# Latent attention with key-major scores and four heads per group, in place of turned probabilities

## The chip, the cores and the metric

The kernel runs on one core of one Trainium2 chip. The metric is the device time of one launch in microseconds. Engines: TensorE (PE, with its weight loads as PEld), VectorE (DVE), ScalarE (ACT), GpSimd (POOL), and SyncE (SP), which issues most DMA transfers. SP's transfers share one queue that is served by the core's 16 DMA engines.

## The reference, cut to what matters

A decoder of two layers works on x of 2 sequences x 1024 tokens x 256 channels. Only the first block is touched by the change, the latent attention of layer 0 (16 heads of 16 channels):

```python
q, k, v = x @ Wq, x @ Wk, x @ Wv                  # x after a layernorm
latent_kv = (k + v) @ W_down_kv                   # 64 latent channels
k_rec, v_rec = latent_kv @ W_up_k, latent_kv @ W_up_v
scores = einsum('bhqd,bhkd->bhqk', heads(q), heads(k_rec)) / 16
scores = clip(scores, -1e4, 1e4)
scores = scores * exp(-1e-4 * abs(i - j))         # i query, j key position
scores = clip(scores, -1e4, 1e4)
out = einsum('bhqk,bhkd->bhqd', softmax(scores), heads(v_rec)) @ Wo
```

The result is added to x. Cross attention, a ternary feed-forward net, feature attention, a second cross attention and routed experts follow; they are as before.

## The kernel before, in words

The program is a row of blocks. Each block holds one instruction list per engine, engines wait for one another by semaphores, and a block ends when all its engines have. Around the change stand, in this order, `normalise`, `latent_projections`, `latent_attention` and `project_out`. The names P = 128, S = 1024, G = 512 (four tiles of 128 tokens), QT = 8 tiles per sequence, HD = 16, H = 16, D = 256 and B = 2 are used throughout.

`latent_projections` makes q and k with channels on the partitions, in 16 pieces of 128 channels x 512 tokens. ScalarE and VectorE split each piece into three bf16 parts whose sum is the fp32 value (L422, L383, L429, L390), and SP stores the parts in DRAM (L445) as `q_parts` and `k_parts`. VectorE takes the largest magnitudes (L385), from which a flag `inside` tells that no score can reach the clip.

`latent_attention` walks over 16 heads x 2 sequences x 8 query tiles, 256 tiles. For each head and sequence, SP loads 12 transfers of 16 rows (L537, L541) into stacks of 96 rows: the six products of parts that count, so that one bf16 matmul gives scores of nearly fp32 precision. Per tile:

- TensorE makes 128 queries x 1024 keys of scores (L578, two matmuls of 512 columns).
- VectorE multiplies by the decay table and takes the maximum of the row in the same instruction (L659, which the profile lists as a custom operation); GpSimd negates that maximum (L563).
- ScalarE takes exp with the negated maximum as bias and sums the row (L706).
- TensorE turns the probabilities, eight fp32 transposes of 128x128 (L588); ScalarE and VectorE copy them from PSUM (L521, L519).
- TensorE multiplies the turned probabilities by the values (L603), four query tiles beside each other in four column groups of 32. This is software pipelined three to eight tiles behind the scores.

Every fourth tile the result is turned back (L612) and divided by the sums (L637, L640). When `inside` is 0 a path with explicit clipping runs instead; the inputs here take the path without it. Last in GpSimd's list stands `clear_slots`, which writes 5 MB of zeros to DRAM (L114, L116), for the routed experts much later.

Of the kernel before, what the change touches and what calls it, by code (L numbers as in the profile page):

```python
# [21 lines left out]
P = 128  # L22
# [279 lines left out]
def latent_projections(k, v_heads, q_scratch, k_scratch):  # L302
# [5 lines left out]
    qk_ready, part1_done, rest1_done, part2_done, part3_done = (  # L308
        k.sem("qk_ready"), k.sem("part1_done"), k.sem("rest1_done"), k.sem("part2_done"), k.sem("part3_done"))
    v_ready, v_done = k.sem("v_ready"), k.sem("v_done")  # L310
    bound_own, largest_ready, largest_turned = k.sem("bound_own"), k.sem("largest_ready"), k.sem("largest_turned")
    stored = [k.sem(f"stored{s}") for s in range(4)]
    scale = 1.0 / 16.0
    NP = NG * 2 * KD
    with ExitStack() as c, nc.Block() as block:
# [3 lines left out]
        parts = k.sb(c, "parts", [P, 4, 3, G], BF16)  # L319
# [7 lines left out]
        def _(pe):  # L327
# [16 lines left out]
            for g in range(NG):  # L344
                rows = slice(g * G, (g + 1) * G)
                for m in range(KD):
                    n = 4 * g + m
                    wait(pe, rest1_done, n - 3)
                    for kd in range(KD):
                        last = pe.matmul(k.ps[:, m, :], k.w["L0_attn_Wq"][:, kd, m * P:(m + 1) * P],  # L350
                                         k.xt[:, kd, rows], start=kd == 0, stop=kd == KD - 1)
                    last.then_inc(qk_ready, 1)
                pe.wait_ge(lat_done, g + 1)
                for m in range(KD):
                    n = 4 * g + 2 + m
                    wait(pe, rest1_done, n - 3)
# [15 lines left out]
        def _(dve):  # L372
# [4 lines left out]
            for g in range(NG):  # L377
                for n in range(4 * g, 4 * g + 4):
                    s = n % 4
                    dve.wait_ge(part1_done, n + 1)  # L380
                    wait(dve, part2_done, n - 3)
                    wait(dve, part3_done, n - 3)
                    dve.scalar_tensor_tensor(out=rest[:, s, :], in0=k.ps[:, s, :], scalar=scale if s < 2 else 1.0,  # L383
                                             in1=parts[:, s, 0, :], op0=ALU.mult, op1=ALU.subtract).then_inc(rest1_done, 1)
                    own.did(dve.tensor_reduce(largest[:, n:n + 1], parts[:, s, 0, :], AX, ALU.max, apply_absolute_value=True))  # L385
                for n in range(4 * g, 4 * g + 4):
                    s = n % 4
                    dve.wait_ge(part2_done, n + 1)
                    dve.wait_ge(rest1_done, n + 1)
                    dve.tensor_tensor(parts[:, s, 2, :], rest[:, s, :], parts[:, s, 1, :],  # L390
                                      ALU.subtract).then_inc(part3_done, 1)

# [15 lines left out]

        @block.scalar  # L410
        def _(act):
# [3 lines left out]

            copy_latent(0)
            for g in range(NG):
                for n in range(4 * g, 4 * g + 4):
                    s = n % 4
                    act.wait_ge(qk_ready, n + 1)  # L420
                    wait(act, stored[s], 16 * g)
                    act.activation(parts[:, s, 0, :], k.ps[:, s, :], ACT.Copy,  # L422
                                   scale=scale if s < 2 else 1.0).then_inc(part1_done, 1)
                if g + 1 < NG:
                    copy_latent(g + 1)
                for n in range(4 * g, 4 * g + 4):
                    s = n % 4
                    act.wait_ge(rest1_done, n + 1)
                    act.activation(parts[:, s, 1, :], rest[:, s, :], ACT.Copy).then_inc(part2_done, 1)  # L429
                for t in range(g * TPG, (g + 1) * TPG):  # L430
                    b, q = divmod(t, QT)
                    act.wait_ge(v_ready, t + 1)
                    act.activation(v_heads[:, b * H:(b + 1) * H, q, :],
                                   k.ps[:, 5 + t % 2, 0:D].rearrange("p (h d) -> p h d", d=HD),
                                   ACT.Copy).then_inc(v_done, 1)

        @block.sync
        def _(sp):
            for n in range(NP):
# [3 lines left out]
                scratch = q_scratch if s < 2 else k_scratch  # L443
                sp.wait_ge(part3_done, n + 1)
                sp.dma_start(scratch[:, b * D + m * P:b * D + (m + 1) * P, half * G:(half + 1) * G]  # L445
                             .rearrange("c p n -> p c n"), parts[:, s, :, :]).then_inc(stored[s], 16)
            for s in range(4):
                sp.wait_ge(stored[s], 16 * NG)

def latent_attention(k, v_heads, attn, decay, q_scratch, k_scratch):

    nc = k.nc
    k.next_block()
    stack_in = [k.sem(f"stack_in{u}") for u in range(2)]
    scored, clipped, peaked, shifted = (  # L460
        k.sem("scored"), k.sem("clipped"), k.sem("peaked"), k.sem("shifted"))
    exp_done, v_staged = k.sem("exp_done"), k.sem("v_staged")
    p_turned = [k.sem(f"p_turned{u}") for u in range(2)]
    pt_done = [k.sem(f"pt_done{u}") for u in range(2)]
    mixed, mix_copied, mix_turned, inverted, weighted = (
        k.sem("mixed"), k.sem("mix_copied"), k.sem("mix_turned"), k.sem("inverted"), k.sem("weighted"))
# [8 lines left out]
    with ExitStack() as c, nc.Block() as block:  # L475
# [18 lines left out]

        def steps(eng, step):

# [1667 lines left out]
```

## Time and profile before

| | |
|---|---|
| median of 3 runs | 1616.47 us (1616.34 to 1617.06) |
| profiled execution, its own time | 1615.76 us |
| its span | 1614.2 us |
| projections block | about 22 to 84 us |
| attention block | 84 to 622 us |
| PE / DVE / ACT / POOL busy over the span | 83% / 57% / 58% / 12% |

In the rows below, times are microseconds from the start of the span. A row of the timeline gives start, duration, engine, line, operation, tiles, shapes, the count of merged instructions, and in brackets how long the engine was idle before and what ended that.
### The profile page before, as it was taken

Reading aid. Unit: us, or ns where it says so; the run is one execution under the profiler, and the core shown is the slowest. Engines: PE = TensorE matmul, PEld = TensorE weight load, DVE = VectorE, ACT = ScalarE, POOL = GpSimd, SP = SyncE. Lnnn points to the kernel's source line nnn. Section 1 sums busy time; section 2 is a strip of 40 time slices with the busy share of each in tenths; the row PEclk is TensorE's granted clock in tenths of the full one; section 3 lists DMA queues with packets and bytes.
Section 4 is the critical chain, followed back from the end, with each engine's and each line's share of the span. In section 5 each row is a group of like instructions: output and inputs, shape, how many; then the busy total and the mean of one; then the engine's idle time right before and its main releaser. Section 6 shows DMA issues by size and latency. Waiting matters only on the chain. (4 is left out here: it accounts for less than half of the span.)

```text
span 1614.2 us, 36474 instructions
## 1 busy us (share of the span) xinstructions
PE 1340.0 (83%) x12288; PEld 960.2 (59%) x12291; DVE 919.8 (57%) x2059; ACT 930.1 (58%) x1793; POOL 190.5 (12%) x546
## 2 busy tenths in 40 slices
PE   5879999999999995898365699889874489999992
PEld 2347777777777774544223464364354279999992
DVE  5558888888888873532788844563354223323233
ACT  2469999999999991355375377624631033333330
POOL 0001111111111110111200000031120701111110
PEclk9879999999999997899756899988995589999996
DMA  3311010010101013200000100033006211111115
GB/s 115 131 51 31 22 27 24 24 26 23 29 20 29 20 38 110 80 1 4 16 1 0 31 1 1 1 120 129 1 4 212 102 34 36 37 36 38 36 33 166
DMA packets 60025, 74.30 MB, mean 46 GB/s; under 512 B 13006, under 2 KB 47728, under 8 KB 59952
## 3 DMA queue, kind: packets, MB, share of 16 engines
q1 hardware_dynamic: 53168, 56.76, 11.9%
q0 software_dynamic: 4672, 14.50, 2.7%
q10 hardware_dynamic: 2112, 2.10, 0.4%
q8 instruction: 43, 0.70, 0.2%
q14 instruction: 30, 0.25, 0.0%
HBM read 50.43 MB, written 22.88 MB: 45 GB/s over the span
## 5 line engine op out<-in xcount | busy, mean ns | idle before, releaser
L659 DVE CUSTOM_DVE_ANT_0 probs_sb<-banks,decay_sb 128x1024 f32<-128x1024 f32 x256 | 308.2, 1221 | 43.6 <-PE banks L578 22.5
L706 ACT ACTIVATE probs_sb<-probs_sb,shift_sb 128x1024 f32<-128x1024 f32 x256 | 294.8, 1151 | 18.1 <-POOL shift_sb L563 16.4
L588 PEld LDWEIGHTS banks<-ident_sb,probs_sb 128*128 128x128 f32 x2048 | 238.3, 141 | 55.1 <-issue 22.9
L588 PE MATMUL banks<-ident_sb,probs_sb 128*128 128x128 f32 x2048 | 267.8, 274 | 0.9 <-ACT probs_t_sb L521 0.8
L521 ACT ACTIVATE probs_t_sb<-banks 128x512 f32<-128x512 f32 x384 | 214.7, 597 | 4.1 <-PE banks L588 2.3
L578 PE MATMUL banks<-k_stack_sb,q_stack_sb 96*128 96x512 bf16 x512 | 156.9, 389 | 14.0 <-DMA k_stack_sb<-k_parts 10.7
L603 PE MATMUL banks<-probs_t_sb,v_head_sb 128*32 128x128 f32 x4096 | 151.2, 277 | 0.7 <-ACT probs_t_sb L521 0.7
L1846 PEld LDWEIGHTS banks<-slots_xt_sb,tile_w_sb 128*128 128x128 f32 x1248 | 146.5, 193 | 1.9
L1846 PE MATMUL banks<-slots_xt_sb,tile_w_sb 128*128 128x128 f32 x1248 | 146.6, 276 | 0.0
L1858 PE MATMUL banks<-experts_w_sb,xt_sb 128*128 x624 | 141.2, 379 | 1.3 <-issue 1.3
L1892 ACT ACTIVATE slots_xt_sb<-banks 128x256 f32<-128x256 f32 x39 | 14.9, 383 | 213.8 <-PE banks L1832 213.8
L1858 PEld LDWEIGHTS banks<-experts_w_sb,xt_sb 128*128 128x128 f32 x624 | 115.5, 190 | 15.8 <-issue 1.7
L519 DVE COPY probs_t_sb<-banks 128x512 f32<-128x512 f32 x128 | 88.6, 692 | 57.7 <-PE banks L588 56.0
L603 PEld LDWEIGHTS banks<-probs_t_sb,v_head_sb 128*32 128x32 f32 x4096 | 100.3, 109 | 32.3 <-issue 31.4
L563 POOL TENSOR_TENSOR shift_sb<-peak_sb,minus_sb 128x1 f32<-128x1 f32 x256 | 48.5, 190 | 452.8 <-DVE peak_sb L659 452.8
L977 DVE TENSOR_REDUCE peak_sb<-banks 128x8 f32<-128x616 f32 x64 | 49.9, 798 | 87.8 <-PE banks L826 87.8
L1019 ACT ACTIVATE pt_sb<-banks,keyfill_sb 77x1024 f32<-77x1024 f32 x64 | 67.5, 1104 | 38.0 <-PE banks L857 37.1
L1902 ACT ACTIVATE xt_sb<-banks,tile_b_sb 128x128 f32<-128x128 f32 x312 | 84.7, 387 | 5.1 <-PE banks L1846 3.4
L1942 DVE COPY tile_w_sb<-experts_w_sb 128x2048 f32 x39 | 47.8, 1227 | 60.2 <-issue 28.0
L1927 DVE TENSOR_TENSOR is_best_sb<-slots_x_sb,tile_owned_sb 128x1 f32<-128x1 f32 x39 | 6.2, 159 | 122.2 <-DMA outputs_y<-slots_y_sb,output_row_sb 122.2
L253 POOL TENSOR_TENSOR x_sb<-x_sb,bb_sb 128x256 f32<-128x256 f32 x48 | 33.0, 732 | 337.2 <-DMA bb_sb<-in_L_attn_bo 276.7
L1881 POOL DMA_INDIRECT outputs_y<-slots_y_sb,output_row_sb x39 | 37.4, 959 | 258.7 <-DVE slots_y_sb L1955 154.0
(289 smaller groups left out, 1910.0 us busy)
## 6 DMA issues: line engine op xcount, KB each, us to landing
experts_w_sb<-in_L_ffn_W SPq DMA_DIRECT2D x16, 1024.0 KB, 11.9
q_stack_sb<-q_parts SPq DMA_DIRECT2D x192, 32.0 KB, 1.7
k_stack_sb<-k_parts SPq DMA_DIRECT2D x192, 32.0 KB, 1.8
slots_x<-zeros_sb POOLq DMA_DIRECT2D x1, 5031.0 KB, 22.6
slots_x_sb<-slots_x SPq DMA_DIRECT2D x39, 129.0 KB, 2.1
xt_sb<-outputs_y SPq DMA_DIRECT2D x8, 512.0 KB, 5.5
q_parts<-parts_sb SPq DMA_DIRECT2D x8, 384.0 KB, 3.0
k_parts<-parts_sb SPq DMA_DIRECT2D x8, 384.0 KB, 4.2
```

Of the source, the lines that this page charges most:

```text
L519: ins = eng.tensor_copy(dst, k.ps[:, 4 + half, :])
L521: ins = eng.activation(dst, k.ps[:, 4 + half, :], ACT.Copy)
L578: last = pe.matmul(k.ps[:, 2 * (s % 2) + half, :], qs[:, u, q * P:(q + 1) * P], ks[:, u, half * 512:(half + 1) * 512], start=True, stop=True)
L588: last = pe.transpose(k.ps[:, 4 + half, j * P:(j + 1) * P], pr[:, s % 4, (half * TPG + j) * P:(half * TPG + j + 1) * P], k.ident[:, :])
L603: last = pe.matmul(k.ps[32 * j:32 * j + 32, 6, 0:P], vh[:, u, kt, :], pt[:, j, gs % 2, kt, :], start=kt == 0, stop=kt == QT - 1)
L659: dve.tensor_tensor_reduce(out=pr[:, s % 4, :], in0=scores, in1=decay[:, off:off + S], scale=1.0, scalar=-3.0e38, op0=ALU.mult, op1=ALU.ma ...
L706: act.activation(pr[:, s % 4, :], pr[:, s % 4, :], ACT.Exp, bias=shift[:, s % 8:s % 8 + 1], accum_out=sums[:, (s // TPG) % 4, s % 4:s % 4 ...
L977: dve.tensor_reduce(peak[:, t % TPG, 2 * half:2 * half + 2, :], k.ps[:, bank:bank + 2, 0:SLOTS * C].rearrange("p r (s n) -> p r s n", n=C) ...
L1019: act.activation(pt[:, n % 2, 2 * half:2 * half + 2, :], k.ps[0:C, 2 * half:2 * half + 2, :], ACT.Exp, bias=key_fill[:, b:b + 1]).then_inc ...
L1846: last = pe.matmul(k.ps[:, 2 * u + f // HALF, (f % HALF) * P:(f % HALF + 1) * P], w1[:, u, kd, f * P:(f + 1) * P], xst[:, u, kd, :], start ...
L1858: last = pe.matmul(k.ps[:, 6, s * D:(s + 1) * D], ht[:, s, f, :], r.w2[:, bass.ds(e, 1), f, :].rearrange("p a n -> p (a n)"), start=f == 0 ...
L1902: ins = act.activation(ht[:, s, f, :], k.ps[:, 2 * s + f // HALF, (f % HALF) * P:(f % HALF + 1) * P], ACT.Gelu_apprx_tanh, bias=b1[:, s, f ...
```

## The change

In `latent_projections`, q and k are each stored in two versions, multiplied by exp(-c n) and exp(+c n) with n the position, so that the product of one version of q with the other of k already carries the decay on one side of the diagonal. That makes 32 rounds instead of 16. GpSimd takes the third part's subtraction. The stacks of the first group are loaded during the last rounds, and the decay tables are loaded here instead of in `normalise`.

In `latent_attention`, work goes in 16 groups: four heads of one sequence x 512 queries. Scores are made twice. The first product, query tile by query tile, serves only to find each row's maximum (`highest`, VectorE; its multiplied scores go to a tile nobody reads); it runs 22 tiles ahead. The maxima of a group are split in three bf16 parts by GpSimd, turned by TensorE, copied, and stored by one transfer as three more rows of the query stack, against rows of -1 in the key stack. The second product has the keys on the partitions, 128 keys x 512 queries, and comes out with the maximum subtracted; ScalarE takes exp of it straight from PSUM and TensorE multiplies it by the values without a turn. A column of ones in the values gives the sums. On diagonal tiles both sides of the diagonal are made and GpSimd's `affine_select` zeroes the wrong half of each. The weights' columns are reordered on the host so that four heads lie together.

Core of the diff (the attention functions are new, so they are shown as they are after it):

```diff
 def latent_projections(k, v_heads, fade_in, stacks, later):
...
+            def apply_fade(e):
+                n, version = divmod(e, 2)
+                dve.wait_ge(qk_ready, n + 1)
+                wait(dve, part3_done, e - 3)
...
+                dve.scalar_tensor_tensor(out=rest[:, e % 4, :], in0=k.ps[:, n % 4, :], scalar=scale if is_query(e) else 1.0,
+                                         in1=fade[:, side, half * G:(half + 1) * G],
+                                         op0=ALU.mult, op1=ALU.mult).then_inc(faded, 1)
+            def subtract_first(e):
...
+        @block.gpsimd
+        def _(pool):
+            for e in range(NV):
+                pool.wait_ge(part2_done, e + 1)
+                pool.wait_ge(rest1_done, e + 1)
+                pool.tensor_tensor(parts[:, e % SLOTS, 2, :], rest[:, e % 4, :], parts[:, e % SLOTS, 1, :],
+                                   ALU.subtract).then_inc(part3_done, 1)
...
+            def first_part(e):
+                act.wait_ge(faded, e + 1)
+                wait(act, stored[e % SLOTS], 16 * (e // SLOTS))      # SLOTS = 6
+                act.activation(parts[:, e % SLOTS, 0, :], rest[:, e % 4, :], ACT.Copy).then_inc(part1_done, 1)
...
+            for e in range(NV):                                      # SP; NV = 32
+                sp.wait_ge(part3_done, e + 1)
+                rows = slice(b * D + m * P, b * D + (m + 1) * P)
+                sp.dma_start(scratch[version, :, half, rows, :].rearrange("c p n -> p c n") if s < 2 else
+                             scratch[version, :, rows, half * G:(half + 1) * G].rearrange("c p n -> p c n"),
+                             parts[:, e % SLOTS, :, :]).then_inc(stored[e % SLOTS], 16)
+                if e == 19:
+                    for x in range(SLOTS):
+                        sp.wait_ge(stored[x], 16 * len(range(x, 16, SLOTS)))
+                if 20 <= e < 26:
+                    load_stacks(sp, stacks, 0, e - 20)
...
+def load_stacks(eng, stacks, g, piece):
+    n, half = divmod(g, 2)
+    b, first = divmod(n * HEADS, H)
+    rows = slice(b * D + first * HD, b * D + (first + HEADS) * HD)
+    version, r = divmod(piece, 3)
+    copies, row = 3 - r, HD * [0, 3, 5][r]
+    dst = slice(row, row + copies * HD)
+    if half == 0:
+        eng.dma_start(stacks.k[dst, n % 2, version, :, :].rearrange("p h n -> p (h n)"),
+                      stacks.k_scratch[version, 0:copies, rows, :].rearrange("c (p h) n -> c p (h n)", h=HEADS)).then_inc(stacks.arrived[g % 3], 16)
+    eng.dma_start(stacks.q[dst, g % 3, version, :, :].rearrange("p h n -> p (h n)"),
+                  stacks.q_scratch[version, r, half, rows, :].rearrange("(p h) n -> p (h n)", h=HEADS)
+                  .unsqueeze(0).to_broadcast([copies, HD, HEADS * G])).then_inc(stacks.arrived[g % 3], 16)
...
 def latent_attention(k, v_heads, attn, decay, inner, stacks):
...
+    GROUPS = 2 * B * H // HEADS      # 16
+    TILES = HEADS * TPG              # 16
+    LEAD = 6
+    TURN_STEP = 5
...
+            def store_peaks(g):
+                sp.wait_ge(peaks_copied, g + 1)
+                sp.dma_start(stacks.q[ROWS:ROWS + PARTS, g % 3, :, :, :].rearrange("p v h n -> p (v h n)"),
+                             peak_rows[:, g % 2, :]).then_inc(peaks_in, 16)
+            for g in range(1, 3):
+                for piece in range(6):
+                    load_stacks(sp, stacks, g, piece)
+            store_peaks(0)
+            for g in range(1, GROUPS):
+                store_peaks(g)
+                if g + 2 < GROUPS:
+                    sp.wait_ge(key_scored, g * UNITS)
+                    for piece in range(6):
+                        load_stacks(sp, stacks, g + 2, piece)
...
+            def scores(tile):                       # TensorE: for the maxima, 1024 columns in 2 or 3 matmuls
+                g, x = divmod(tile, TILES)
+                h, j = divmod(x, TPG)
+                if x == 0:
+                    stacks_arrived(pe, stacks, g)
+                wait(pe, peaked, tile - 1)
...
+            def key_scores(g, i, h):                # TensorE: 128 keys x 512 queries, banks 4 to 6 in a ring
+                if i == 0 and h == 0:
+                    pe.wait_ge(peaks_in, (g + 1) * 16)
+                wait_for_bank(pe, item)
...
+            def sum_values(s):
+                pe.wait_ge(exp_done, unit_index(g, i, HEADS if on_diagonal(i) else HEADS - 1) + 1)
+                if on_diagonal(i):
+                    pe.wait_ge(selected, s // 2 + 1)
...
+            pe.wait_ge(constants, 2)
+            for tile in range(TILES + LEAD):
+                scores(tile)
+                if tile == TILES + 1:
+                    turn_peaks(0)
+            for g in range(GROUPS):
+                for i in range(QT):
+                    if g * QT + i >= 2:
+                        sum_values(g * QT + i - 2)
+                    for x in range(2):
+                        for h in range(2 * x, 2 * x + 2):
+                            key_scores(g, i, h)
+                        if x == 1 and i == TURN_STEP and g + 1 < GROUPS:
+                            turn_peaks(g + 1)
+                        if tile_at(g, i, x) < GROUPS * TILES:     # (g + 1) * TILES + 2 * i + LEAD + x
+                            scores(tile_at(g, i, x))
+                    if on_diagonal(i):                            # i odd
+                        diagonal_scores(g, i)
+                    if i == 3 and g > 0:
+                        turn_mix(g - 1)
...
+        def _(pool):
+            own.did(pool.memset(vh[:, :, :, :, :], 0.0))          # 128 x 2048 fp32
+            own.wait()
+            pool.memset(stacks.k[ROWS:ROWS + PARTS, :, :, :, :], -1.0).then_inc(constants, 1)   # 3 x 16384 bf16
+            pool.wait_ge(constants, 1)
+            pool.tensor_copy(ident_b[:, :], k.ident[:, :]).then_inc(constants, 1)
...
+            def select(g, i):
+                pool.wait_ge(exp_done, unit_index(g, i, HEADS - 1) + 1)
+                pool.affine_select(later, later, [[0, HEADS], [1, P]], ALU.is_ge, 0.0, base=0, channel_multiplier=-1)
+                pool.wait_ge(exp_done, unit_index(g, i, HEADS) + 1)
+                pool.affine_select(earlier, earlier, [[0, HEADS], [-1, P]], ALU.is_gt, 0.0, base=0,
+                                   channel_multiplier=1).then_inc(selected, 1)
...
+            def exponential(g, i, h):                             # ScalarE, 576 times 128 x 512
+                act.wait_ge(key_scored, u + 1)
+                act.wait_ge(released, u + 1)
+                act.activation(out, k.ps[:, bank_of((exp_done, u + 1)), :], ACT.Exp).then_inc(exp_done, 1)
```

Values are multiplied two steps after their exps. The stacks have three slots for queries and two for keys. A group with an even number loads both, one with an odd number only queries.

## Rows read from the trace of the kernel before

**Rows 1.** The page's part 1: busy time and share of the span.

```profile
PE 1340.0 (83%) x12288; PEld 960.2 (59%) x12291; DVE 919.8 (57%) x2059; ACT 930.1 (58%) x1793; POOL 190.5 (12%) x546
```

**Rows 2.** Busy time in the attention loop, with its columns.

```profile
core 0: us, PE busy (x) PEld busy (x) DVE busy (x) ACT busy (x) POOL busy (x), PEclk, DMA share, GB/s
...
92.00:608.00 516.00, 509.02 (x6718) 375.47 (x6716) 412.60 (x768) 496.98 (x960) 58.90 (x289) 0.99 0.11 27
```

**Rows 3.** Timeline of PE in steady state.

```profile
299.93 0.61 PE L578 MATMUL banks<-k_stack_sb,q_stack_sb 96*128 96x512 bf16 x2
300.38 1.04 PE L588 MATMUL banks<-ident_sb,probs_sb 128*128 128x128 f32 x8
301.34 0.65 PE L603 MATMUL banks<-probs_t_sb,v_head_sb 128*32 128x128 f32 x16
301.92 0.60 PE L578 MATMUL banks<-k_stack_sb,q_stack_sb 96*128 96x512 bf16 x2
...
304.75 0.86 PE L603 MATMUL banks<-probs_t_sb,v_head_sb 128*32 128x128 f32 x24
305.55 0.60 PE L578 MATMUL banks<-k_stack_sb,q_stack_sb 96*128 96x512 bf16 x2
```

**Rows 4.** Groups by line and form: busy us, mean ns, idle before.

```profile
L659 DVE CUSTOM_DVE_ANT_0 probs_sb<-banks,decay_sb 128x1024 f32<-128x1024 f32 x256 | 308.2, 1221 | 43.6 <-PE banks L578 22.5 <-issue 13.7 <-PE banks L588 4.4
L706 ACT ACTIVATE probs_sb<-probs_sb,shift_sb 128x1024 f32<-128x1024 f32 x256 | 294.8, 1151 | 18.1 <-POOL shift_sb L563 16.4
L521 ACT ACTIVATE probs_t_sb<-banks 128x512 f32<-128x512 f32 x384 | 214.7, 597 | 4.1 <-PE banks L588 2.3
L1482 ACT ACTIVATE l_pj_sb<-banks,l_bk_sb 128x512 f32<-128x512 f32 x8 | 5.5, 685 | 6.6 <-PE banks L1369 6.6
L253 POOL TENSOR_TENSOR x_sb<-x_sb,bb_sb 128x256 f32<-128x256 f32 x48 | 33.0, 732 | 337.2 <-DMA bb_sb<-in_L_attn_bo 276.7 <-DMA bb_sb<-in_L_xattn_bo 60.5
L936 POOL TENSOR_TENSOR peakparts_sb<-peakrest_sb,peakparts_sb 128x16 bf16<-128x16 f32 x32 | 7.1, 220 | 2.6
L559 POOL COPY v_head_sb<-v_heads_sb 128x128 f32 x28 | 8.1, 289 | 3.2 <-issue 3.1
...
L923 POOL MEMSET peakparts_sb<- 128x1024 bf16 x2 | 2.4, 1178 | 70.8 <-POOLq L160 70.8
...
L548 POOL MEMSET v_head_sb<- 128x512 f32 x1 | 0.5, 524 | 84.9 <-issue 84.9
...
L549 POOL MEMSET minus_sb<- 128x1 f32 x1 | 0.1, 98 | 0.0
```

**Rows 5.** Timeline where the attention block starts.

```profile
83.99 2.67 SPq L537 DMA_DIRECT2D q_stack_sb<-q_parts  x6
...
90.91 1.89 PE L578 MATMUL banks<-k_stack_sb,q_stack_sb 96*128 96x512 bf16 x4 [10.71 <-DMA k_stack_sb<-k_parts]
```

**Rows 6.** Timeline where it ends, and the queue's row of its last transfer.

```profile
607.51 0.22 DVE L640 TENSOR_TENSOR attn_sb<-banks,inv_sb 128x64 f32<-128x64 f32 x1 [3.04 <-PE banks L612]
622.20 3.27 PEld L261 LDWEIGHTS banks<-ident_sb,attn_sb 128*128 128x128 f32 x16 [14.98 <-issue]
...
slots_x<-zeros_sb POOLq DMA_DIRECT2D x1, 5031.0 KB, 22.6
```

**Rows 7.** Timeline of ACT and DVE in the projections.

```profile
31.37 0.60 ACT L422 ACTIVATE parts_sb<-banks 128x512 bf16<-128x512 f32 x1 [1.32 <-PE banks L350]
...
36.10 0.68 DVE L383 SCALAR_TENSOR_TENSOR rest_sb<-banks,parts_sb 128x512 f32<-128x512 f32 x1
36.70 0.68 DVE L385 TENSOR_REDUCE largest_sb<-parts_sb 128x1 f32<-128x512 bf16 x1
...
76.80 2.49 DVE L390 TENSOR_TENSOR parts_sb<-rest_sb,parts_sb 128x512 bf16<-128x512 f32 x4
```

**Rows 8.** Packets of the DMA queues in 0.5:10.9 and in 643:653.5.

```profile
DMA packets 2400, 2.17 MB, mean 208 GB/s; under 512 B 224, under 2 KB 2400, under 8 KB 2400
...
DMA packets 2113, 1.38 MB, mean 132 GB/s; under 512 B 627, under 2 KB 2112, under 8 KB 2112
```

**Rows 9.** Windows while large loads run, columns as in rows 2.

```profile
3.00:9.00 6.00, 0.00 (x0) 0.00 (x0) 3.95 (x12) 0.00 (x0) 0.00 (x0) 1.00 1.07 348
1087.00:1092.00 5.00, 4.61 (x46) 2.70 (x47) 2.41 (x4) 0.93 (x2) 0.83 (x4) 1.00 1.03 413
```

**Rows 10.** Timeline of PE in the cross attention.

```profile
702.86 1.06 PE L871 MATMUL banks<-pt_sb,va_sb 77*32 77x512 f32 x8
703.86 0.30 PE L821 MATMUL banks<-hidden_sb,fillb_sb 3*128 3x308 bf16 x2
```

**Rows 11.** Window in the projections after a pause of PE, columns as in rows 2.

```profile
41.80:46.20 4.40, 4.40 (x6) 1.85 (x6) 0.00 (x0) 0.92 (x2) 0.00 (x0) 0.50 0.60 195
```

More of the change, by code:

```diff
@@ L376, in _ @@
             dve.tensor_copy(wkv[:, :, :], k.ps[:, 7, 0:KD * L].rearrange("p (m n) -> p m n", m=KD)).then_inc(wkv_done, 1)
[L377 to L391, printed above, removed]
+            def apply_fade(e):
+                n, version = divmod(e, 2)
+                dve.wait_ge(qk_ready, n + 1)
+                wait(dve, part3_done, e - 3)
+                side = version if is_query(e) else 1 - version
+                half = n // 4 % 2
+                dve.scalar_tensor_tensor(out=rest[:, e % 4, :], in0=k.ps[:, n % 4, :], scalar=scale if is_query(e) else 1.0,
+                                         in1=fade[:, side, half * G:(half + 1) * G],
+                                         op0=ALU.mult, op1=ALU.mult).then_inc(faded, 1)
@@ L394, in _ @@
+            for e in range(NV + 1):
+                if e < NV:
+                    apply_fade(e)
+                if e > 0:
+                    subtract_first(e - 1)
             own.wait()
@@ L438, in _ @@
         def _(sp):
-            for n in range(NP):
+            for v in range(2):
+                sp.dma_start(fade[:, v, :], fade_in[v].partition_broadcast(P)).then_inc(fade_arrived, 16)
+            later.start(sp)
+            for e in range(NV):
+                n, version = divmod(e, 2)
                 g, s = divmod(n, 4)
@@ L442, in _ @@
                 m = s % 2
[L443 to L451, printed above, removed]
+                scratch = stacks.q_scratch if s < 2 else stacks.k_scratch
@@ new lines, in _ @@
+                if 20 <= e < 26:
+                    load_stacks(sp, stacks, 0, e - 20)
+            for x in range(SLOTS):
+                sp.wait_ge(stored[x], 16 * len(range(x, NV, SLOTS)))
+            later.wait(sp)
+class Stacks:
+    pass
+HEADS = 4
+def load_stacks(eng, stacks, g, piece):
[11 more added lines that the diff above has]
+                  .unsqueeze(0).to_broadcast([copies, HD, HEADS * G])).then_inc(stacks.arrived[g % 3], 16)
@@ L457, in latent_attention, with stacks_arrived @@
+def stacks_arrived(eng, stacks, g):
+    eng.wait_ge(stacks.arrived[g % 3], 16 * sum(6 if x % 2 else 12 for x in range(g % 3, g + 1, 3)))
+def latent_attention(k, v_heads, attn, decay, inner, stacks):
     nc = k.nc
     k.next_block()
[L459 to L463, printed above, removed]
@@ new lines, in split_peaks @@
+            def split_peaks(g):
+                parts = [peak_parts[:, g % 2, r, :, :] for r in range(PARTS)]
+                both = peak[:, g % 2, :].unsqueeze(1).to_broadcast([P, 2, TILES])
+                pool.wait_ge(peaked, (g + 1) * TILES)
+                wait(pool, peaks_turned, g - 1)
+                own.did(pool.tensor_copy(parts[0], both))
+                own.wait()
+                own.did(pool.tensor_tensor(peak_rest[:, :, :], both, parts[0], ALU.subtract))
+                own.wait()
+                own.did(pool.tensor_copy(parts[1], peak_rest[:, :, :]))
+                own.wait()
+                pool.tensor_tensor(parts[2], peak_rest[:, :, :], parts[1], ALU.subtract).then_inc(peaks_split, 1)
+                pool.wait_ge(peaks_split, g + 1)
@@ new lines, in _ @@
+            own.wait()
+            stage_values(0)
+            split_peaks(0)
+            for g in range(GROUPS):
+                for i in range(QT):
+                    if on_diagonal(i):
+                        select(g, i)
+                    if i == 3 and g % 2 == 0 and g + 2 < GROUPS:
+                        stage_values(g // 2 + 1)
+                    if i == TURN_STEP - 1 and g + 1 < GROUPS:
+                        split_peaks(g + 1)
+            clear_slots(k, pool, zeros_set)
```

545 lines of the change are left out of this document (313 added, 232 removed).

## The prediction

> **What bounds the kernel now.** I read the page first, then the busy time by stage, then one steady step of TensorE in order of time, then the groups by form, then the two ends of the attention block, and last the packets of the DMA queue.
>
> The page has TensorE at 83% with VectorE and ScalarE far below, but that is a mean over stages [rows 1]. By stage, the attention loop from 92 to 608 us is a third of the span. There TensorE is busy 509.0 of 516 us and ScalarE 497.0, VectorE 412.6, and the DMA engines move 27 GB/s [rows 2]. The steady steps tell what TensorE's time is made of [rows 3]. Two score matmuls of 512 columns take 0.45 us (299.93 to 300.38), eight transposes 0.96, 16 value matmuls 0.58 and 24 of them 0.80. A run of 4 query tiles is 4x0.45 + 4x0.96 + 0.58 + 2x0.80 = 7.8 us, and 64 of them make 500 of the loop's 516 us. So TensorE is the bound, ScalarE (exp of 1024 elements 1151 ns, copies of turned probabilities 597 ns) is close behind [rows 4], and half of TensorE's time is the transposes. Both go with the change. Around the loop lie 6.9 us from the block's start to the first matmul and 14.7 us from the last VectorE operation to the next block, the latter behind a 5 MB transfer that GpSimd issues at its end, and that takes 22.6 us from issue to landing [rows 5, 6].
>
> **1. Projections.** Each of 16 pieces is now made in two faded versions: 32 rounds of scale, copy, subtract, copy, subtract, store. VectorE does five operations of 512 elements per two rounds, at 0.60 us each when back to back (36.10 to 36.70) and 0.68 with their ends [rows 7]: 1.50 to 1.70 us a round, I take 1.65. GpSimd's subtraction of 512 is bounded by its 256-element one, 732 ns, and its 16-element one, 220 ns [rows 4]: 1.28 us, under VectorE's time. ScalarE's first copy starts at 31.4 us [rows 7]; 31.4 + 32x1.65 = 84.2, plus copy and GpSimd 2.6, plus the 4.7 us that end the block now (79.3 to 84.0): 91.7, so +7.7 us.
>
> **2. How the new loads are cut.** The old stacks came in transfers of 16 rows. The new ones have, for the three and two copies, a source whose outermost count is 3 or 2 (times 16 rows), going to 48 or 32 partitions. Which engines work on that is the whole question. Every transfer that finishes leaves small packets, one per engine. At the start six transfers of 128 rows leave 224 packets under 512 B, of which 128 are the rows of the head mask: 96 = 6x16. At 643 us eleven transfers leave 627, of which 256 + 128 + 77 are rows of two biases and two masks: 166 = 9x16 + 2x11 [rows 8]. The two odd ones are the value bias and the key mask, with 77 rows each. 77 was cut in 11 equal shares, the largest number up to 16 that divides it, not in 16 unequal ones. So a transfer is cut into equal shares along its outermost count. No transfer here has different counts on its two sides; equal cuts of a list of 3 blocks can give no more than 3 shares, and I take 3 and 2 engines, the same first ones each time. The other end is 16 engines (a cut by target partitions), kept as a rival.
>
> The Trainium skill, page DMA: Bandwidth & Descriptors, section Why a DMA increments its semaphore by 16 and not by 1, says that the engines used are the largest number up to 16 that divides the slowest count of both sides; its section Rules for kernel authors adds that a leading broadcast of c copies confines a transfer to c engines. By it the sum is the one below; by a cut on the target side alone it would be the rival's. The trace agrees in 11 shares for 77 rows; the unequal sides no row shows.
>
> Price: 413 GB/s with all 16 engines full is 25.8 GB/s for one [rows 9]. An even group (keys and queries) puts on the first engine, for two versions, (393,216 + 196,608)/3 + (262,144 + 131,072)/2 + (131,072 + 65,536)/16 = 405,504 B, so 811,008 B: 31.4 us. An odd group (queries alone) 270,336 B: 10.5 us.
>
> **3. Backlog in the projections.** The stacks of group 0 are issued from round 20 on, near 31.4 + 33 + 4.2 = 68.6 us, between stores of which each needs that engine too (384 KB/16: 0.95 us). ScalarE's first copy of round 31 waits for the store of round 25, which stands behind five of the six pieces (30.9 us) and six stores (5.7): 70 + 36.6 = 106.6. With the chain of that round (3.2) and the end of the block (4.7, hops 0.4) the block ends at 114.9 instead of 84.0: +30.9 us (this holds step 1; without the cut +7.7).
>
> **4. Attention block, start.** TensorE waits for GpSimd to write constants: 2048 fp32 and 16,384 bf16 elements in 3 partitions. Rows of 524 ns for 512 fp32 and 1178 ns for 1024 bf16, less the 0.1 us that each memset costs whatever its size, make 0.83 and 1.05 ns per element [rows 4], so 1.8 + 17.3 us, with 1.3 us of entry and the identity's copy 20.7 us, against 6.9 now. Then 22 tiles run ahead at VectorE's pace, 1.22 us a tile [rows 4] with some overlap, I take 1.2: the first key product comes 25 us later, at 45.7. The other way to it is 18 transfers (41.9 us on the first engine) and the peak rows behind them: 46.5. I take 46.5.
>
> **5. The loop.** Per two key tiles TensorE has 4 tiles of 1024 columns (1.8 us), 8 key products (1.8), 4 small ones (0.4), and twice the values: 8 matmuls of 512 columns and 32 rows out take 1.00 us in the cross attention (702.86 to 703.86 [rows 10]), plus 0.22 once for the diagonal. That is 6.2; weights of the small ones load behind long ones, so 6.1. ScalarE: 9 exps of 512 from PSUM, 0.55 to 0.69 us each (a copy 597 ns, a form with a bias operand 685 [rows 4]): 5.0 to 6.2, I take 5.2, under TensorE. VectorE: 4x1.22 = 4.9 [rows 4]. GpSimd: two selections of 512 elements, not in this trace; the copy (289 ns for 128 [rows 4]) gives 0.6 us if 0.2 of it is fixed, as in the 16-element row, and the two-input operation gives 1.28. The values of a step come a full step (2.8 us) after its end, the fourth exp ends 0.6 us after it: 2.1 us with the hops, so up to 1.05 us each is free. I take 0.6 to 1.0, since it has one input. A group is 4x6.1 + 0.6 of turns + 0.7 (TensorE waits for peaks that are taken and split only then) = 25.7 us; 16 groups less 5 us, because the last tiles are already done: 406.
>
> **6. Stall on the loads.** Loads of group g+2 are issued when group g starts and TensorE asks for them at its sixth step, 17.4 us in (three steps of 2.85, two of 3.35, a turn of 0.5, then values and two key products). The odd ones are there. The even ones end at 1.9 + 31.4 = 33.3: 15.9 us of stall, in groups 2, 4, ... 12; TensorE works in order, so what stands behind that wait, key products included, waits too, and with them ScalarE. Each stall lets the clock fall: in the projections, where TensorE had just paused for ScalarE's copies, the granted clock is 0.50, 1.2 of 2.4 GHz, through 4.4 us of solid matmuls [rows 11], 2.2 us lost. Less the 0.7 that it covers: 17.4 x 6 = 104 us.
>
> **7. End.** Last exps 1.0, selection 0.7, then clearing the slots 0.65 + 22.6 + 0.35 (today partly under the loop's end): 25.3 us.
>
> Attention block: 46.5 + 406 + 104 + 25.3 = 581.8 against 538.2 now (83.99 to 622.20): +43.6; with step 3, +74.5. Span 1614.2 becomes 1688.7, the profiled run 1615.76 becomes 1690.3, and the median of the runs, 0.7 above it, 1691 us.
>
> **Rivals.** (a) All 16 engines carry the loads. Then 2.36 MB take 6 us, steps 3 and 6 vanish: 7.7 + 45.7 + 406 + 25.3 - 538.2 = -53.5, so 1563 us, faster. For it: 48 target partitions could be cut evenly by 16, and the loop has DMA room. Against it: the 11 shares. It decides at an even load of about 20 us: stall (4.5 us, six times) and backlog then eat most of the 53 us. (b) The selection costs the two-input price, 1.28 us: the values wait 0.46 us per pair of steps, 64 times, less what the stalls cover: +24, 1715 us, slower. A group is then over 27 us even when odd. (c) ScalarE at 0.69 us per exp is level with TensorE, +10 us or so; in the ranges.
>
> **Numbers.** Forecast 0.70, (a) 0.20, (b) 0.08, anything else (a cheap stall, level) 0.02. The forecast's own range: an ideal TensorE and no slow clock take off 38, an engine at 22 GB/s adds 50 (the loads of 1 KB rows at the start have 348 GB/s, 21 per engine or less [rows 9]): 1655 to 1745. It leaves 3 in 10 out with (a), so the range is 1550 to 1745. What a measurement can tell from no change is about 0.2%. Faster is (a), 0.20; slower the forecast and (b), 0.78; same 0.02.
>
> **What would show it.** Right: loads of three copies landing after tens of us; about 18 us of TensorE idle in every even group, ended by the stacks' DMA; a clock of 0.5 just after; ScalarE waiting for stores late in the projections; a DMA share near 0.15 while the loads run. Wrong: landings of 2 to 8 us and groups all of 26 us, which is (a); idle before value matmuls ended by GpSimd, which is (b). Key score matmuls near 0.22 us apart and 19 us of GpSimd's memset test steps 4 and 5 by themselves.

## The result and the profile after

The changed kernel takes 1743.9 us (median of 4 runs, 1742.7 to 1745.5) against 1616.4: ratio 1.0789, 95% interval 1.077 to 1.0808, slower. The prediction said 1691 in a range of 1550 to 1745, slower with chance 0.78. Direction and mechanism held; the size fell 53 us short, and the time lies 1.1 us inside the upper end of the range. The profiled execution took 1742.8 us, with a span of 1741.1.

The page's part 1, to be held against [rows 1]: nobody is near full any more.

```profile
PE 1278.7 (73%) x8848; PEld 762.1 (44%) x8851; DVE 851.4 (49%) x1867; ACT 762.0 (44%) x1473; POOL 288.2 (17%) x492
```

TensorE's longest waits in the attention block (engine, line and what ended the wait: us, times, longest), and then the place in group 2 where it stands still, in order of time (SP's rows from one view, TensorE's from another):

```profile
PE banks L644 <- DMA q_stack_sb<-q_parts: 119.1, 6, 20.7
PE banks L651 <- DMA q_stack_sb<-peak_rows_sb: 4.2, 1, 4.2
PE banks L700 <- POOL peak_parts_sb L763: 3.0, 10, 0.3
PE banks L651 <- ACT xt_sb L914: 2.6, 9, 0.6
PE banks L689 <- POOL probs_d_sb L774: 1.0, 1, 1.0
```

```profile
230.23 0.69 SPq L516 DMA_DIRECT2D k_stack_sb<-k_parts  x1
...
241.38 4.66 SPq L518 DMA_DIRECT2D q_stack_sb<-q_parts  x1
...
247.38 0.61 PE L651 MATMUL banks<-q_stack_sb,k_stack_sb 99*128 99x256 bf16 x4
268.67 1.03 PE L644 MATMUL banks<-k_stack_sb,q_stack_sb 96*128 96x128 bf16 x3 [20.68 <-DMA q_stack_sb<-q_parts]
...
279.76 3.71 SPq L518 DMA_DIRECT2D q_stack_sb<-q_parts  x6
```

SP's first load row marks a group's start, so group 2 runs from 230.23 to 279.76, 49.5 us. Its loads are issued from 230.23 on, SP itself takes 4.66 us over one issue, and TensorE asks at 248.0 and gets its stacks at 268.67. The windows show the engines:

```profile
core 0: us, PE busy (x) PEld busy (x) DVE busy (x) ACT busy (x) POOL busy (x), PEclk, DMA share, GB/s
204.20:230.20 26.00, 25.54 (x209) 10.49 (x213) 19.77 (x35) 19.22 (x39) 5.84 (x12) 1.00 0.10 32
238.20:240.20 2.00, 2.00 (x23) 0.79 (x21) 1.42 (x3) 1.86 (x4) 0.25 (x1) 1.00 0.19 59
244.20:246.20 2.00, 2.00 (x17) 0.76 (x15) 1.27 (x5) 1.45 (x4) 0.76 (x2) 1.00 0.20 82
254.00:268.00 14.00, 0.00 (x0) 0.00 (x0) 0.00 (x0) 0.00 (x0) 0.00 (x0) 0.50 0.12 49
268.60:279.80 11.20, 11.13 (x70) 4.99 (x74) 5.84 (x9) 5.80 (x12) 1.27 (x2) 0.70 0.02 4
```

A DMA share of 0.19 is 3 of 16 engines, 0.12 is 2. If the transfers with two source blocks ran on engines of their own, the share would be 0.31 where both kinds are queued; but for the short transfers of 16 rows it stays at 0.20 or less, so they share the same ones. While two engines worked at 49 GB/s, TensorE did nothing for 14 us; then it worked on at half clock until about 275 us (mean 0.70 to the group's end). An odd group takes 26.0 us, and TensorE is busy for 25.5 of it. The operations that the trace of before didn't have, from the page's costliest groups:

```profile
L914 ACT ACTIVATE xt_sb<-banks 128x512 f32<-128x512 f32 x344 | 179.6, 602 | 164.7 <-PE banks L651 164.7
...
L771 POOL TENSOR_SCALAR_AFFINE_SELECT xt_sb<-xt_sb 128x512 f32<-128x512 f32 x43 | 27.3, 635 | 271.7 <-ACT xt_sb L914 271.7
...
L435 POOL TENSOR_TENSOR parts_sb<-rest_sb,parts_sb 128x512 bf16<-128x512 f32 x32 | 41.1, 1301 | 85.2 <-ACT parts_sb L451 85.2
```

At the two ends of the block and before it (ACT, POOL, PE and PEld in order of time):

```profile
96.29 0.63 ACT L447 ACTIVATE parts_sb<-rest_sb 128x512 bf16<-128x512 f32 x1 [3.94 <-DMA k_parts<-parts_sb]
103.61 0.63 ACT L447 ACTIVATE parts_sb<-rest_sb 128x512 bf16<-128x512 f32 x1 [6.17 <-DMA k_parts<-parts_sb]
114.93 0.63 ACT L447 ACTIVATE parts_sb<-rest_sb 128x512 bf16<-128x512 f32 x1 [8.37 <-DMA q_parts<-parts_sb]
123.36 0.63 ACT L447 ACTIVATE parts_sb<-rest_sb 128x512 bf16<-128x512 f32 x1 [7.01 <-DMA q_parts<-parts_sb]
...
130.57 3.73 SPq L518 DMA_DIRECT2D q_stack_sb<-q_parts  x6
133.73 13.75 POOL L741 MEMSET k_stack_sb<- 3x16384 bf16 x1
179.33 1.03 PE L651 MATMUL banks<-q_stack_sb,k_stack_sb 99*128 99x512 bf16 x2 [4.20 <-DMA q_stack_sb<-peak_rows_sb]
...
748.22 3.27 PEld L261 LDWEIGHTS banks<-ident_sb,attn_sb 128*128 128x128 f32 x16 [20.36 <-issue]
```

The projections end at 130.5 us (before: 84.0). The attention block takes 617.7 us (130.5 to 748.2; before: 538.2).

### The profile page after: what moved, and what is told of

Same layout as the page of the kernel before. It is cut to its first block and busy times, and to the rows that moved or that the text cites. A ratio compares the mean times of both kernels' runs of the same rounds, so it can differ in the third digit from the quotient of the medians.

```text
span 1741.1 us, 26064 instructions
## 1 busy us (share of the span) xinstructions
PE 1278.7 (73%) x8848; PEld 762.1 (44%) x8851; DVE 851.4 (49%) x1867; ACT 762.0 (44%) x1473; POOL 288.2 (17%) x492
## 5 line engine op out<-in xcount | busy, mean ns | idle before, releaser
L815 DVE CUSTOM_DVE_ANT_0 faded_scores_sb<-banks,inner_sb 128x1024 f32<-128x1024 f32 x256 | 304.8, 1223 | 251.0 <-PE banks L644 249.9
L644 PE MATMUL banks<-k_stack_sb,q_stack_sb 96*128 96x512 bf16 (+3 forms) x704 | 169.8, 349 | 145.7 <-DMA q_stack_sb<-q_parts 119.1
L914 ACT ACTIVATE xt_sb<-banks 128x512 f32<-128x512 f32 x344 | 179.6, 602 | 164.7 <-PE banks L651 164.7
L651 PE MATMUL banks<-q_stack_sb,k_stack_sb 99*128 99x128 bf16 (+3 forms) x960 | 186.2, 304 | 10.0 <-DMA q_stack_sb<-peak_rows_sb 4.2
L644 PEld LDWEIGHTS banks<-k_stack_sb,q_stack_sb 96*128 96x128 bf16 x704 | 67.0, 103 | 210.9 <-DMA q_stack_sb<-q_parts 120.7
L651 PEld LDWEIGHTS banks<-q_stack_sb,k_stack_sb 99*128 99x128 bf16 x960 | 74.5, 100 | 170.1 <-ACT xt_sb L914 66.0
L914 ACT ACTIVATE probs_sb<-banks 128x512 f32<-128x512 f32 x168 | 87.6, 603 | 75.4 <-PE banks L651 75.4
L692 PE MATMUL banks<-xt_sb,v_head_sb 128*32 128x512 f32 x688 | 93.0, 613 | 0.0
L771 POOL TENSOR_SCALAR_AFFINE_SELECT xt_sb<-xt_sb 128x512 f32<-128x512 f32 x43 | 27.3, 635 | 271.7 <-ACT xt_sb L914 271.7
L435 POOL TENSOR_TENSOR parts_sb<-rest_sb,parts_sb 128x512 bf16<-128x512 f32 x32 | 41.1, 1301 | 85.2 <-ACT parts_sb L451 85.2
```

The source lines that it names most:

```text
L435: pool.tensor_tensor(parts[:, e % SLOTS, 2, :], rest[:, e % 4, :], parts[:, e % SLOTS, 1, :], ALU.subtract).then_inc(part3_done, 1)
L644: last = pe.matmul(k.ps[:, 2 * (tile % 2) + half, lo - half * G:hi - half * G], stacks.q[0:ROWS, g % 3, version, h, j * P:(j + 1) * P], st ...
L651: return pe.matmul(k.ps[:, bank, at:at + hi - lo], stacks.k[0:ROWS + PARTS, g // 2 % 2, version, h, kt * P:(kt + 1) * P], stacks.q[0:ROWS ...
L692: last = pe.matmul(k.ps[VW * h:VW * (h + 1), PV_BANK, :], vh[:, n % 2, h, kt, :], probs_of(s)[:, h, :], start=i == 0, stop=i == QT - 1, sk ...
L815: dve.tensor_tensor_reduce(out=junk[:, tile % 2, :], in0=tile_scores(tile), in1=inner[:, window(tile)], scale=1.0, scalar=-3.0e38, op0=ALU ...
L914: act.activation(out, k.ps[:, bank_of((exp_done, u + 1)), :], ACT.Exp).then_inc(exp_done, 1)
```

## The experiments

The kernels ran in four groups, each beside runs of the kernel before on its own chip: the changed kernel (before: 1616.4 us), how the loads are cut (1612.5), the other steps (1612.3) and the rest (1612.6). Between groups it is the ratios to the kernel before that are compared. A difference between two of the kernels is uncertain by about 5 us.

**How the loads are cut.** Four kernels, the first with nothing changed but the order in which the rows of a segment are walked:

```diff
-  stacks.k_scratch[version, 0:copies, rows, :].rearrange("c (p h) n -> c p (h n)", h=HEADS))
+  stacks.k_scratch[version, 0:copies, rows, :].rearrange("c (p h) n -> p c (h n)", h=HEADS))
...
-  .unsqueeze(0).to_broadcast([copies, HD, HEADS * G]))
+  .unsqueeze(1).to_broadcast([HD, copies, HEADS * G]))
```

> Same transfers, same bytes, same SP instructions; only the order in which the rows of a three- or two-copy segment are walked is turned, 16 channels outermost and the copies inside. Theory (a transfer is cut along its outermost count, so three copies ride on three engines): an even group's 2.36 MB now lie on 16 engines, 147 KB each, at the 21 GB/s per engine of the changed kernel 7 us instead of 38.4; the six waits of TensorE for the stacks (119 us) and the slow clock behind them (6 x 2.9) go, and the projections block ends near 108 instead of 130.5 us, since its rounds by themselves take 2.4 us. 1744 - 136 - 22 = about 1586 us. Rival (the volume, the queue or SP's issuing is what is slow, not the cut): no change, 1744 us, six waits of 20 us as before.

In the second, third and fourth every copy is a transfer of its own, for both stacks, for the keys alone and for the queries alone (the counts that TensorE waits for follow):

```diff
-        eng.dma_start(stacks.k[dst, ...], stacks.k_scratch[version, 0:copies, rows, :]...)
+        for c in range(copies):
+            eng.dma_start(stacks.k[row + c * HD:row + (c + 1) * HD, ...], stacks.k_scratch[version, c, rows, :]...)
```

> Every copy is a transfer of its own from 16 rows, 24 instead of 12 transfers in an even group, 12 instead of 6 in an odd one. Theory: as with 16 rows outermost, about 1586 us, and SP's issuing (24 x 0.4 to 0.7 us, 10 to 17 us) ends just before TensorE asks, 17.8 us into the group; so 1586 to 1600. Rival (number of transfers and SP's issuing set the pace): slower than the changed kernel, over 1750 us.

> Only the key transfers are split by copy. Theory: the first engine carries 270,336 B of queries and 1/16 of 1,572,864 B of keys, 368,640 B in an even group: 17.5 us at 21 GB/s, and about 20 with issue and landing, against a question at 17.8 us: waits of 2 to 3 us in each even group, projections block ended near 110: about 1602 us. Rival (volume): 1744 us, or above it for six more issues a group.

> Only the query transfers are split by copy. Theory: the first engine carries 540,672 B of keys and 1/16 of 786,432 B of queries, 589,824 B: 28 us, so waits of 11 to 12 us in each even group and a slow clock behind them still, projections block ended near 120: about 1680 us. Rival (volume): 1744 us.

Measured (load: the 17.8 us from a group's start until TensorE asks, and its mean wait):

| kernel | us | ratio to before | first engine carries | wait, 6 times | load |
|---|---|---|---|---|---|
| changed | 1743.9 | 1.0789 | 811,008 B | 119.1 | 37.7 |
| queries apart | 1690.7 | 1.0492 [1.047, 1.0514] | 589,824 B | 79.7 | 31.1 |
| keys apart | 1651.5 | 1.0252 [1.0226, 1.0279] | 368,640 B | 50.6 | 26.2 |
| both apart | 1599.0 | 0.993 [0.9903, 0.9957] | 147,456 B | 11.3 | 19.7 |
| 16 rows outermost | 1579.4 | 0.9797 [0.9774, 0.982] | 147,456 B | 0 | under 17.8 |

The rival by volume, number of transfers or issuing is out: same bytes, same number of transfers and issues, and 9.2% less time. In the waits view of the first no wait for stacks is left, and its windows (columns as above; the keys-apart kernel in the second fence) show the whole load over 16 engines:

```profile
204.60:218.60 14.00, 13.85 (x110) 5.37 (x110) 10.94 (x21) 10.56 (x21) 3.46 (x6) 1.00 0.95 162
204.60:230.60 26.00, 25.54 (x209) 10.56 (x213) 19.68 (x35) 19.21 (x39) 6.39 (x13) 1.00 0.55 93
```

```profile
PE banks L645 <- DMA q_stack_sb<-q_parts: 50.6, 6, 9.2
...
217.60:219.60 2.00, 2.00 (x23) 0.75 (x21) 1.48 (x3) 1.79 (x4) 0.19 (x1) 1.00 1.06 129
225.60:227.60 2.00, 1.73 (x20) 0.58 (x20) 1.66 (x4) 1.01 (x3) 0.21 (x1) 1.00 0.21 78
229.60:231.60 2.00, 0.00 (x0) 0.00 (x0) 0.00 (x0) 0.00 (x0) 0.00 (x0) 0.60 0.13 53
```

16 rows outermost came 7 us under its expectation, both apart inside it, queries apart 11 us over. The miss is keys apart, 49 us over. I had let the part on 16 engines run at 16 times one engine's rate. It goes at 129 GB/s in the window shown (104 to 152 in those around it), so 1.57 MB of keys take about 12.2 us, and the queries' 10.5 us on 3 and 2 engines (the prediction's price) come on top of it. The 3.5 us that are missing to 26.2 I put down to start and landing; they weren't measured by themselves.

**Where the volume sits.** Why do 16 busy engines move 162 GB/s only, where [rows 9] have 348 and 413? Two kernels on top of 16 rows outermost: keys in packets of 4 KB, and keys read three times from one place.

```diff
+        for x in range(0, HEADS, 2):
+            eng.dma_start(stacks.k[dst, n % 2, version, x:x + 2, :]..., stacks.k_scratch[...][:, :, x:x + 2, :]...)
```

```diff
+        eng.dma_start(stacks.k[dst, ...], stacks.k_scratch[version, 0, rows, :]....unsqueeze(1).to_broadcast([HD, copies, HEADS * S]))
```

> On top of the kernel with 16 rows outermost, the key rows of 8 KB go in two transfers of 4 KB each, as the query rows do. There an even group's 2.36 MB took 15 us at about 165 GB/s on 16 engines that were all busy, an odd group's 0.79 MB 4 us at up to 229. If the 8 KB packets are what is slow: keys and queries at 200 to 230 GB/s, 10 to 12 us, landings of 3 to 5 instead of 7 to 8.5 us. If it is the volume that queues up (issuing outruns the engines): 15 us as before. The time of the kernel stays 1579 us either way.

> On top of the kernel with 16 rows outermost, all copies of the keys are read from the first of the three stored parts, so the sums leave the smaller parts out. A transfer then reads its rows three times from one place, as the queries' does, and not from three places 1 MB apart. If the distance of the places is what keeps 16 engines at 165 GB/s: 200 to 230 GB/s and 10 to 12 us for an even group. If not: 15 us. Kernel time 1579 us either way.

1580.0 and 1580.1 us, one time each. Windows of the one and of the other:

```profile
202.20:216.20 14.00, 13.85 (x111) 5.39 (x110) 10.94 (x21) 10.59 (x21) 3.45 (x6) 1.00 0.86 162
```

```profile
204.70:219.00 14.30, 14.15 (x112) 5.43 (x108) 11.21 (x22) 10.50 (x21) 3.83 (x7) 1.00 0.91 164
```

Neither shortens the load. The distance of the sources is out: with one place in place of three, 16 engines are as busy (0.91) and as slow. Packet size is not settled. The kernel with 4 KB packets makes 18 issues, the last of which ends 11.9 us into the load, which is as long as its theory gives the whole load (10 to 12 us), and its engines are busy for 0.86 of the window and not 0.95, so SP's issuing may hold that load by itself. What caps the rate stays open. The stacks' transfers write to 16 to 48 of the 128 partitions, and no kernel was made to test that. One row bears on it: both apart moves the same bytes from the same places, but every one of its transfers writes 16 partitions, and 16 busy engines then move 132 GB/s over the whole load and not 162. Their number doubles as well, so the row alone does not decide.

```profile
204.40:222.40 18.00, 17.62 (x139) 6.75 (x139) 13.92 (x26) 13.03 (x26) 4.43 (x8) 1.00 0.97 132
```

**The other steps, each by itself**, on top of 16 rows outermost:

```diff
                 if g + 1 < NG:
                     latent(g + 1)
+                    queries(g + 1)          # the Wq matmuls, moved from the head of the next turn
                 for j in range(TPG):        # the values
```

> On top of the kernel with 16 rows outermost, TensorE makes the query pieces of the next 512 tokens before the values of these, so that it doesn't stand with them behind ScalarE's copies of the values. Theory (the rounds take 2.4 instead of 1.65 us because the next pieces come late, 4.1 us of VectorE's and ScalarE's idle time at each of three changes of piece group): 3 x 4.1 = 12 us off the projections block, 1579 to about 1567 us. Rival (the chain of five steps over three engines sets the rounds): no change, 1579 us.

```diff
         def _(pool):                        # projections
+            pool.memset(stacks.k[6 * HD:6 * HD + 3, :, :, :, :], -1.0).then_inc(ones_set, 1)
+            pool.wait_ge(ones_set, 1)
...
-            pool.memset(stacks.k[ROWS:ROWS + PARTS, :, :, :, :], -1.0).then_inc(constants, 1)     # attention
```

> On top of the kernel with 16 rows outermost, GpSimd writes the -1 of the three extra key rows at the start of the projections block, where it idles until 34.9 us, and not at the start of the attention block. Theory (TensorE's 22 us wait there is this memset of 13.75 us): it ends near 36.5, so the first subtraction is 1.6 us later; 12 to 13.75 us less, about 1567 us. Rival (the stacks of groups 0 to 2, which land until 127 us, hold the start as well): under 3 us less.

```diff
             for g in range(GROUPS):         # attention, GpSimd
+                if g == 1:
+                    clear_slots(k, pool, zeros_set)
...
-            clear_slots(k, pool, zeros_set)
```

> On top of the kernel with 16 rows outermost, GpSimd issues the 5 MB of zeros at the start of group 1 and not after the last group. Theory (the block's end waits for that transfer alone): the 20 us between the last division and the next block go but for 1 to 2, about 1560 us. Rival (the 5 MB collide with the stacks of an even group, which need 15 us for themselves of the 17.8 that TensorE gives them): one wait of 5 to 20 us comes back, 1565 to 1580 us.

> 16 rows outermost, the values later, the -1 early and the zeros early together. If the three parts lie at three different places they add up: 1579 - 12 - 12 - 19 = about 1536 us, 0.95 of the kernel before. If the early memset delays rounds that no longer have slack: 1540 us.

| kernel | us | ratio to before | against 16 rows outermost |
|---|---|---|---|
| values later | 1575.4 | 0.9771 [0.9752, 0.979] | -4 |
| -1 early | 1570.4 | 0.9738 [0.972, 0.9755] | -9.5 |
| zeros early | 1564.0 | 0.9706 [0.9686, 0.9725] | -15 |
| all three | 1546.8 | 0.9595 [0.9576, 0.9614] | -33 |

The parts add up within the noise: 4 + 9.5 + 15 = 28.5, measured 33. All three together are 4% faster than the kernel before and beat the changed kernel by 11%. Each gives less than its expectation (12, 12 to 14 and about 19 us; together 1547 for 1536). Values later is not clear of noise by its time: its interval overlaps the 0.9774 to 0.982 of 16 rows outermost. Its trace does show an effect. ScalarE's waits for a faded piece in the kernel without and with it (the same operation, L452 in the second):

```profile
ACT parts_sb L447 <- DVE rest_sb L395: 18.6, 13, 4.1
```

```profile
ACT parts_sb L452 <- DVE rest_sb L400: 8.0, 8, 3.0
```

From first to last fade, 31 rounds take 68.8 us (32.1 to 100.9) without it and 59.2 (31.5 to 90.7) with it, 2.22 and 1.91 us a round. So the late pieces cost 0.31 us a round. The 1.91 that are left I put down to the chain over three engines; that wasn't tested by itself, and eight of the waits are still there. The median shows only 4 us of these 9.6: from the first fade to GpSimd's first memset of the attention block it is 78.7 and 71.4 us, 7.3 less, and the runs spread over 6 us without it and 3 with it. -1 early takes TensorE's wait for the constants from 22.2 to 8.6 us, zeros early its wait at the block's end from 18.9 to 3.5 (16 rows outermost, then -1 early and zeros early):

```profile
PE banks L644 <- POOL ident_b_sb L743: 22.2, 1, 22.2
PE banks L261 <- PEq L587: 18.9, 1, 18.9
```

```profile
PE banks L647 <- POOL ident_b_sb L744: 8.6, 1, 8.6
```

```profile
PE banks L261 <- PEq L587: 3.5, 1, 3.5
```

**The selection**, made twice (no value changes):

```diff
+                own.did(pool.affine_select(later, later, ...))
+                own.wait()
                 pool.affine_select(later, later, ...)
```

> On top of the kernel with 16 rows outermost, every selection on GpSimd is made twice, which changes no value: four of 0.63 us for a diagonal step in place of two. Theory (the values' matmuls have about 1 us to spare behind the second selection): 1.3 to 1.4 us more against 1, so 0.4 us of waiting of TensorE, 64 times, 1579 + 27 = about 1606 us. Rival (GpSimd is off the path by more than that): 1579 us.

1599.2 us, 0.9917 [0.9898, 0.9937], so about +20. A wait that was 1.0 us in all is now a stall:

```profile
PE banks L689 <- POOL probs_d_sb L779: 18.1, 33, 2.4
```

It comes in 33 of 64 steps and not in all: the spare time differs from step to step. The direction is the theory's, the size three quarters of it (20 of 27 us). At one selection each GpSimd has room enough, but in about half the steps less than the 1.3 us that the second ones add.

**The first load**, behind the last store, in the changed kernel:

```diff
-                if 20 <= e < 26:
-                    load_stacks(sp, stacks, 0, e - 20)
...
+            for piece in range(6):
+                load_stacks(sp, stacks, 0, piece)
```

> The changed kernel, but the stacks of group 0 are issued behind the last store of the projections and not between them. Theory (from the first load to the first key product the first engine is never idle: 88 us for three groups' stacks and the stores between): the block ends near 109 again, but the 88 us start at 104.5, so the first key product comes at 193 instead of 179: +14, about 1758 us. Rival (the peaks' own chain sets the start: block end, 36 us for group 0, 25 us of tiles): 176 to 179, so 1741 to 1744 us.

1751.0 us, 1.0875 [1.0844, 1.0905], against 1.0789: +7 to +14 us. The first key product comes at 190.77 instead of 179.33 us and again waits for the peak rows' transfer, now 17.7 us. TensorE's wait for group 0's stacks is now 43.6 us, and the DMA share from 105 to 190.7 us is 0.19. So from the first load to the first key product it is the few engines of these loads that set the pace, and loading early gains only what they would idle. The block did not end near 109 but at 125, since SP was held in its own issues until 123.9: the engines' backlog reaches SP.

## Why the prediction was right, and where it was short

Its own sum was 1688.7 us of span, the profile has 1741.1: 52.4 us more. The table's differences make 51.5 of them, the blocks behind it 0.9. The range held the time by 1.1 us, and that is partly luck: its upper end was made of engines at 22 GB/s, and what filled it was also step 1, whose rounds were 17.7 us too short and which no part of the range allowed for. The terms (16 rows outermost shows each step without the cut):

| step | predicted | changed kernel | 16 rows outermost |
|---|---|---|---|
| 1, 3: projections end | 114.9 | 130.5 | 109.4 |
| 4: block start to first key product | 46.5 | 48.8 | 44.4 |
| 5: loop without the stalls | 406 | | 414.8 |
| 6: stalls and slow clock | 104 | 132.6 | 0 |
| 7: end | 25.3 | 21.5 | 20.2 |

(132.6 is the changed loop's 547.4 us, from the first key product at 179.3 to the end of the last value matmul at 726.7, less the 414.8, 153.8 to 568.6, of the kernel without stalls. The six even groups that stall are together 132.6 us longer than six of 26.0, which agrees.)

- **Step 1, mis-sized.** Rounds were priced at 1.65 us by VectorE's work alone. They take 2.22: 0.31 more for TensorE, whose next pieces stand behind the values' matmuls, which wait for ScalarE, and 0.26 that I put down to the chain over three engines without a test. Without a backlog the block ends at 109.4, not 91.7.
- **Step 2, right.** Shares of 0.19 and 0.12 are 3 and 2 engines, and turning the order of the rows removes them. The rule of the Trainium skill, page DMA: Bandwidth & Descriptors, section Why a DMA increments its semaphore by 16 and not by 1, is that the engines are the largest number up to 16 that divides the slowest count of both sides; the trace agrees, now on transfers with 48 target partitions and an outermost source count of 3 too. A cut by the source's outermost count alone would fit the same rows; no run here tells the two apart.
- **Step 3, right.** Backlog 21.1 us (130.5 - 109.4) against 23.2 (114.9 - 91.7).
- **Step 4, right within 2.3 us.** Memset 13.75 us, not 17.3: 0.84 ns per element as in the fp32 row, not 1.05. With the backlog the peak rows' transfer is the last thing waited for (4.2 us), without it the memset's chain.
- **Step 5, right in the group, 8.8 us short in all.** A group takes 26.0 us against 25.7, the same in both kernels: about 5 us over 16 groups. The rest lies in the 5 us taken off for tiles already done, of which 1.5 came. ScalarE's exp, 0.60 us, and the selection, 0.63, were inside their bounds, so rivals (b) and (c) are out. Selecting twice shows what (b) would have done: 20 us more where it said 24.
- **Step 6, mis-sized, the largest miss.** The mean wait is 19.9 us against 15.9, because the load takes 37.7 us from the group's start and not 33.3. The price per engine was right for the stall (49 GB/s on two, 25 each), but earlier three engines moved 59 to 82 GB/s, 20 to 27 each. Behind each wait 2.3 us more are lost ((132.6 - 119.1)/6), net of whatever the wait covers; the prediction's net was 1.5, a slow clock of 2.2 less 0.7 covered.
- **Step 7, 4 to 5 us too dear.** The zeros set it, as zeros early shows, but the last exps and selections were added ahead of them and lie inside the loop: GpSimd's memset for the zeros starts at 725.25, 1.5 us before the last value matmul ends.
- **Rival (a)** is not what the changed kernel does, but with the rows turned it is what happens: 1579 us against its 1563, on a chip where the kernel before takes 4 us less. Steps 1 and 5 were 17.7 and 8.8 us short, step 7 was 5.1 too dear. Its load takes about 15 us, not 6, and both apart, with a load of 19.7 us, comes out 0.7% under the kernel before, where I had put its point of decision at 20.

## What to carry to other kernels

Before counting a load's bytes, count the engines that its outermost dimension can be cut over: here a leading dimension of 3 or 2 copies put it on 3 or 2 engines, and the same rows walked the other way round went over 16 and took 9% off the kernel. Price a chain of rounds not only by its busiest engine: follow the dependency through all of them, and ask what stands ahead of the work that feeds it. Constants and clears that nobody needs yet belong where their engine idles.

## What was not expected of the hardware

- Sixteen busy engines moved 129 to 164 GB/s for these stacks, 8 to 10 each, where two or three moved 20 to 27 each. The cause is open.
- An issue on SP, 0.4 to 0.7 us when the engines keep up, took up to 9.7 us when they were behind.
- Short waits can cost more than themselves, and their length alone does not tell which. The six waits of both apart were 1.8, 2.2, 1.5, 1.9, 2.0 and 1.8 us. Behind the first the granted clock stayed at 1.00 and the group took 27.6 us. Behind the second it fell to 0.50 for about 6 us, and the group took 30.9 us, 2.7 more than 26.0 and the wait. The next three kept 1.00; the last, of 1.82 us, lost 1.3. What decides between them, no run here shows. The first, second and last of these groups:

```profile
204.40:232.00 27.60, 25.67 (x209) 10.54 (x213) 19.60 (x35) 19.23 (x39) 6.35 (x13) 1.00 0.64 88
258.00:289.00 31.00, 28.66 (x210) 11.80 (x213) 19.77 (x35) 19.52 (x39) 6.39 (x13) 0.89 0.58 78
...
476.08:505.19 29.11, 27.14 (x209) 11.29 (x213) 19.77 (x35) 19.35 (x39) 6.39 (x13) 0.94 0.60 83
```
